# Multiplying y batch by batch in two row tiles of TensorE

## The chip, the cores and the metric

The kernel runs on one core of a Trainium2 chip. The metric is the device time of one launch in microseconds (us). Two runs of the kernel before took 425.37 and 426.58 us; their median, 425.98 us, is the time that the prediction starts from. The engines are named PE (TensorE matmuls), PEld (TensorE weight loads, which overlap PE), DVE (VectorE), ACT (ScalarE), POOL (GpSimd) and SP (SyncE, here for DMA issues only).

## What is computed

```python
# x: (64, 64, 1024) = (B, C, T); condition: (64,), values 0..15; weights: (16, 64, 64)
W = weights[condition]
y = jnp.einsum('bct,bcd->bdt', x, W)                 # one 64 x 64 matrix for each batch
x_flat = y.reshape(-1, 1024)                         # (4096, 1024)
top1 = jnp.argmax(x_flat @ gate_w.T + expert_bias, axis=-1)
base_out = jnp.einsum('bth,oh->bto', y, W_up)        # W_up: (1024, 1024)
z = jnp.einsum('nh,erh->ner', x_flat, lora_A)        # 4 experts of rank 8
delta = (z @ lora_B of expert top1) * SCALE
out = x + base_out + delta
```

All in float32. The first step, y, is what the change is about: 64 products of a batch's own 64 x 64 matrix with its 64 x 1024 slice of x.

## The kernel before

**Blocks.** The 64 batches are worked in 16 blocks of four. A block has two tiles (t = 0, 1), each of two batches that lie on 128 partitions: batch 0 of the pair on partitions 0 to 63, batch 1 on 64 to 127. Blocks 0 and 1 are partly written out on their own; blocks 2 and 3, a hardware loop over pairs (even, odd), and the last two blocks follow.

**y.** `make_y(q, par, t, h)` (L779) makes half h of y of tile t for block q, while the block ahead of it is multiplied. It has four matmuls, each with 128 columns of x as the stationary operand and `cond_pair` as the moving one. `cond_pair` is 128 x 128 and block-diagonal: the two matrices of the pair stand in its corners and zeros elsewhere, so one matmul makes y for both batches. The result, transposed (128 positions of T by 2 x 64), goes into one bank of the two-bank `y_ps`, half h into bank h. Plain float32 matmuls appear in the trace as two weight loads and two matmul records each, so a `make_y` call is 8 of each. There are four calls to a block, at four places, and 14 blocks in which y is made so (for blocks 2 to 15): 56 calls. Blocks 0 and 1 have their y from `make_first_y` (L790), which is not changed. ACT then copies the bank to SBUF (`move_y`, L522) as operand a11, a12, a21 or a22 and counts `y_summed`.

**The product with W_up.** It is done by a Strassen-like scheme: seven half-size products of a block (a11, a12, a22, s1, s2, s3, s4; `multiply`, L855), with sums of operands on POOL (L302 to L317) and operands split in a high part (ACT, L533) and a low part (DVE, L289). For an odd block and the even one ahead of it, product a22 is done in quarters (q1 to q7, L1071). In these, operands are of the type fp32r, and each matmul is one load and one matmul record. Results are added to x in SBUF by DVE (L1264, L1268, L1458) and stored by SP.

**The expert path.** DVE finds the best expert of each row in six small steps and leaves `z_parts` (L1251). PE transposes it (`turn_z`, L884), ACT copies it to `z_t` (`move_z`, L611), and PE adds the expert's part to the products' banks (`add_delta`, L875). This is done twice for each block: `turn_z` with `delta11_of` and `delta12_of` for tile 0, and `turn_second_z` with `second_delta` for tile 1. In the kernel before, the fourth `make_y` stands between `turn_second_z` and `second_delta`.

**Order.** The order on each engine is written out by hand and kept by semaphores: `y_done` (PE has made a half), `y_summed` (ACT has moved it), `z_turned`, `z_ready` (z copied), `low["s4"]` (a12 may be overwritten), `c11_out`, `u3_out` and others for banks that DVE has emptied. Each engine works in its own order, so whatever stands behind a wait waits too.

Of the kernel before, what the change touches and what calls it, by code (L numbers as in the profile page):

```python
# [5 lines left out]
def adaln_ffn_kernel(  # L6
# [62 lines left out]
    with ctx:  # L69
# [189 lines left out]
        def t_place(k, c):  # L259

            return {1: t_sb[:, c, :], 2: b12_sb[:, c, :], 3: bank_of(("b11", c)), 4: bank_of(("b21", c))}[k]

        def raw_slot(row):
            return row // OH * 2 + row % 2
# [244 lines left out]
        def _(act):  # L509
# [198 lines left out]
            def one(q):  # L708
                load_x(q + 1, 0, 0)
                round_s1(q, True)  # L710
                round_s2(q, True)
                load_x(q + 1, 0, 1)
                round_s4(q, True)
                round_s3(q, True)
                move_z(q, 1, 0, bank_c[:, 0, :])
                move_y(q + 1, 0, 0, a11)
# [4 lines left out]
                move_y(q + 1, 1, 0, a21)  # L721
                move_z(q, 1, 1, chains[0][:, 1, :])
# [6 lines left out]
                move_y(q + 1, 1, 1, a22_even)  # L729

            def even(q, g):
                load_x(q + 1, 1, 0)
                round_s1(q, True)
                round_s2(q, True)
                load_x(q + 1, 1, 1)
                round_s3(q, True)
                round_s4(q, True)
                round_even_a22(q, g)
                move_z(q, 0, 0, bank_c[:, 0, :])
                move_y(q + 1, 0, 0, a11)  # L740
                round_a11(q + 1, True)
                act.wait_ge(low["s4"], q + 1)
                move_y(q + 1, 0, 1, a12)
                round_a12(q + 1, True)
                move_y(q + 1, 1, 0, a21)
                move_z(q, 0, 1, chains[1][:, 1, :])
                move_y(q + 1, 1, 1, a22)

            def odd(q, g, closing):
                if not closing:  # L750
                    load_x(q + 1, 0, 0)
                round_s1(q, True)
                round_quarter(5, g)
                round_s2(q, True)
                round_quarter(6, g)
                round_quarter(3, g)
# [4 lines left out]
                if not closing:  # L761
                    move_y(q + 1, 0, 0, a11)
                    round_a11(q + 1, True)
                move_z(q, 1, 0, y_ps[:, 1, :])
                if not closing:
                    act.wait_ge(low["s4"], q + 1)
                    move_y(q + 1, 0, 1, a12)
                    round_a12(q + 1, True)
                    move_y(q + 1, 1, 0, a21)
                move_z(q, 1, 1, chains[0][:, 1, :])  # L770
                if not closing:
                    move_y(q + 1, 1, 1, a22_even)

# [4 lines left out]
        def _(pe):  # L778
            def make_y(q, par, t, h):  # L779
                if h == 0:  # L780
                    pe.wait_ge(x_loaded[2 * par + t], 8 * (q - par) + 16)
                    pe.wait_ge(pair_loaded[2 * par + t], 16 * (q - par) + 32)
                pe.wait_ge(y_summed, 4 * q + 2 * t + h - 1)
                for k in range(KH):
                    mm = pe.matmul(y_ps[:, h, k * P:(k + 1) * P],  # L785
                                   x_sb[:, 2 * par + t, (h * KH + k) * P:(h * KH + k + 1) * P],
                                   cond_pair[:, 2 * par + t, :], start=True, stop=True)
                mm.then_inc(y_done, 1)

# [92 lines left out]
            def turn_z(dst, q, t):  # L882
                pe.wait_ge(route_step, ROUTE_STEPS * (2 * q + t + 1))
                pe.transpose(dst, z_parts[:, :, :].rearrange("p n q -> p (n q)"), ident[:, :]).then_inc(z_turned, 1)  # L884

            def delta11_of(q, pair):
# [128 lines left out]
            def one(q):  # L1015
# [8 lines left out]
                multiply("s2", q, chain, False)  # L1024
                make_y(q + 1, 0, 0, 0)
                pe.wait_ge(p4_out, q)
# [3 lines left out]
                delta11_of(q, pair)  # L1030
                make_y(q + 1, 0, 0, 1)
                pe.wait_ge(u2_out, q + 1)
                multiply("s3", q, chain, False)
                make_y(q + 1, 0, 1, 0)
                multiply("s4", q, bank_c, True)
                delta12_of(q)
                turn_second_z(q, pair)
                make_y(q + 1, 0, 1, 1)
                pe.wait_ge(u3_out, q + 1)
                second_delta(q, chain)  # L1040

            def even(q, g):
# [72 lines left out]
            def odd(q, g, closing):  # L1115
                chain, pair = chains[1], chains[0]
                first_quarters(q, g, chain, pair)
                if closing:
                    close(q, g, chain, pair)
                    return  # L1120
                make_y(q + 1, 0, 0, 0)
                pe.wait_ge(quarter_out, quarters(g, 3))
                multiply("s1", q, bank_b, True)
                pe.wait_ge(y_summed, 4 * q + 4)
                turn_z(y_ps[:, 1, 0:P], q, 0)
# [3 lines left out]
                make_y(q + 1, 0, 0, 1)  # L1129
# [4 lines left out]
                make_y(q + 1, 0, 1, 0)  # L1134
# [4 lines left out]
                make_y(q + 1, 0, 1, 1)  # L1139
                pe.wait_ge(u3_out, q + 1)  # L1140
# [409 lines left out]
```

## Time and profile before

| | |
|---|---|
| times of the two runs | 425.37 and 426.58 us, median 425.98 |
| span of the profiled execution | 423.9 us, so 1.4 to 2.6 us of a run lie around the span |
| PE busy | 414.2 us (98%), 3003 matmul records |
| PEld busy | 393.6 us (93%) |
| DVE / ACT / POOL busy | 280.3 / 146.0 / 137.3 us |
| chain of waits that ended last | PE 92% |
| matmul records of y at L785 | 448, in 14 blocks |
| mean granted TensorE clock | 0.996 of 2.4 GHz |

A busy time is the union of the records of a group. Matmul records overlap each other, since their recorded length holds the way through the array, so the distance from start to start, not the length, tells what one costs. For weight loads the same holds. Idle time of an engine that nobody waits for costs nothing.

### The profile page before, as it was taken

To read this page: it belongs to the slowest core of one execution; us is meant where nothing else is said; L and a number is where in the kernel's file an instruction comes from. 1 tells how busy PE (TensorE), PEld (TensorE's weight loads), DVE (VectorE), ACT (ScalarE), POOL (GpSimd) and SP (SyncE) were. 2 spreads that over 40 slices of the span, in tenths; PEclk is the share of its full clock that TensorE was granted. 3 is DMA by queue.
4 is the path that set the end of the run, shared out by engine and by line. 5 is a ranking of instruction groups with operands and counts; after the bars stand their busy time and mean duration, and the time that the engine had idled before them with its cause. 6 is when DMAs were issued, how large, how long until landed. Compare 5 with 4: busy or idle time off the path is not lost.

```text
span 423.9 us, 8776 instructions
## 1 busy us (share of the span) xinstructions
PE 414.2 (98%) x3003; PEld 393.6 (93%) x3003; DVE 280.3 (66%) x605; ACT 146.0 (34%) x282; POOL 137.3 (32%) x123
## 2 busy tenths in 40 slices
PE   7998999999999999999999999999999999999997
PEld 6897998999999999999999999999999999999996
DVE  4699668586756576474675656575764756856684
ACT  5795222433223242232333233232332323323320
POOL 1488215506204080312605053050802216050430
PEclk9899999999999999999999999999999999999999
DMA  8820230503114032321125021150322212240102
GB/s 269 302 65 2 89 117 26 178 27 106 67 57 159 26 107 100 105 76 74 56 99 176 28 102 38 65 179 25 105 97 82 99 55 75 99 177 29 49 26 100
DMA packets 20991, 39.36 MB, mean 93 GB/s; under 512 B 7494, under 2 KB 7750, under 8 KB 20970
## 3 DMA queue, kind: packets, MB, share of 16 engines
q1 hardware_dynamic: 17600, 27.40, 18.3%
q10 hardware_dynamic: 3370, 11.69, 8.1%
q8 instruction: 12, 0.20, 0.2%
q14 instruction: 9, 0.07, 0.1%
HBM read 22.30 MB, written 16.78 MB: 92 GB/s over the span
## 4 chain that ended last, share of the span: by engine, by line
PE 92%; DVE 3%; DMA 1%; ACT 1%; SPq 1%; issue 1%; POOL 1%; ACTq 0%; POOLq 0%
PE bank_y L869 21%; PE bank_x L869 21%; PE y_ps L785 11%; PE bank_b L869 10%; PE bank_c L869 10%; PE bank_c L1071 5%; PE bank_b L1071 4%; DMA x_sb<-in_x_dram 1%; PE bank_x L849 1%; PE y_ps L794 1%; PE bank_x L875 1%; PE bank_b L875 1%; PE bank_y L875 1%; PE bank_c L875 1%; PE y_ps L1147 1%
## 5 line engine op out<-in xcount | busy, mean ns | idle before, releaser
L524 ACT ACTIVATE a<-y_ps 128x512 f32<-128x512 f32 x49 | 29.3, 598 | 93.4 <-PE y_ps L785 93.4
L785 PE MATMUL y_ps<-cond_pair,x_sb 128*128 128x128 f32 x448 | 59.0, 274 | 0.0
L785 PEld LDWEIGHTS y_ps<-cond_pair,x_sb 128*128 128x128 f32 x448 | 54.7, 191 | 1.2
L869 PE MATMUL bank_y<-w_s,hl_s 128*128 128x292 f32 (+1 forms) x384 | 51.4, 289 | 0.0
L869 PE MATMUL bank_x<-w_a,hl_a 128*128 128x256 f32 (+1 forms) x384 | 50.9, 288 | 0.0
L869 PEld LDWEIGHTS bank_x<-w_a,hl_a 128*128 128x128 f32 x384 | 49.5, 188 | 0.3
L304 POOL TENSOR_TENSOR s_sum<-a 128x512 f32<-128x512 f32 x9 | 11.6, 1291 | 117.3 <-ACT a L524 115.1
L869 PEld LDWEIGHTS bank_y<-w_s,hl_s 128*128 128x128 f32 x384 | 49.2, 188 | 0.1
L869 PE MATMUL bank_b<-w_s,hl_s 128*128 128x512 f32 x192 | 47.9, 398 | 0.0
L869 PE MATMUL bank_y<-w_a,hl_a 128*128 128x292 f32 x360 | 47.7, 288 | 0.0
L869 PEld LDWEIGHTS bank_y<-w_a,hl_a 128*128 128x128 f32 x360 | 46.6, 188 | 0.3
L869 PE MATMUL bank_x<-w_s,hl_s 128*128 128x292 f32 x336 | 45.2, 290 | 0.4 <-DVE hl_s L289 0.4
L304 POOL TENSOR_TENSOR s_sum<-a,a_even 128x512 f32<-128x512 f32 x7 | 9.0, 1291 | 112.4 <-ACT a_even L524 112.4
L869 PE MATMUL bank_c<-w_s,hl_s 128*128 128x512 f32 x180 | 45.0, 398 | 0.0
L869 PEld LDWEIGHTS bank_x<-w_s,hl_s 128*128 128x128 f32 x336 | 43.0, 188 | 0.6 <-issue 0.6
L869 PEld LDWEIGHTS bank_b<-w_s,hl_s 128*128 128x128 f32 x192 | 35.0, 188 | 6.9
L869 PEld LDWEIGHTS bank_c<-w_s,hl_s 128*128 128x128 f32 x180 | 32.7, 188 | 6.6 <-issue 0.2
L289 DVE TENSOR_TENSOR hl_s<-s_sum,hl_s 128x512 fp32r<-128x512 f32 x30 | 36.3, 1246 | 1.2 <-ACT hl_s L533 1.2
L289 DVE TENSOR_TENSOR hl_a<-a,hl_a 128x512 fp32r<-128x512 f32 x31 | 21.3, 689 | 18.9 <-ACT hl_a L533 18.9
L533 ACT ACTIVATE hl_s<-s_sum 128x512 fp32r<-128x512 f32 x32 | 20.2, 634 | 34.1 <-POOL s_sum L304 24.7
L1264 DVE TENSOR_TENSOR x_sb<-bank_y,x_sb 128x512 f32<-128x512 f32 x40 | 27.3, 682 | 6.0 <-PE bank_y L875 4.8
L533 ACT ACTIVATE hl_s<-a 128x512 fp32r<-128x512 f32 x32 | 19.3, 628 | 33.4 <-POOL a L312 22.5
(187 smaller groups left out, 648.3 us busy)
## 6 DMA issues: line engine op xcount, KB each, us to landing
out_dram<-x_sb SPq DMA_DIRECT2D x63, 256.0 KB, 2.0
x_sb<-in_x_dram ACTq DMA_DIRECT2D x22, 512.0 KB, 3.5
x_sb<-in_x_dram SPq DMA_DIRECT2D x10, 512.0 KB, 3.4
w_raw<-in_L_ffn_W_up_dram SPq DMA_DIRECT2D x8, 512.0 KB, 6.3
cond_pair<-in_L_cond_weights_dram SPq DMA_DIRECT2D x64, 16.0 KB, 2.2
out_dram<-x_sb SPq DMA_DIRECT2D x2, 128.0 KB, 2.0
router_sb<-in_L_ffn_lora_A_dram ACTq DMA_DIRECT2D x1, 128.0 KB
lora_b_sb<-in_L_ffn_lora_B_dram SPq DMA_DIRECT2D x1, 128.0 KB, 4.9
```

The costliest lines, as they stand in the source:

```text
L289: eng.tensor_tensor(hl[op][:, 1, :, :], by_k(src[:, :]), hl[op][:, 0, :, :].bitcast(fp32), ALU.subtract)\
L304: eng.tensor_tensor(s1_sum[:, :], a21[:, :], second[:, :], ALU.add).then_inc(s1_added, 1)
L524: act.activation(to[:, :], y_ps[:, h, :], ACT.Copy).then_inc(y_summed, 1)
L533: act.activation(hl[op][:, 0, :, :], src[:, :].rearrange("q (k n) -> q k n", n=P), ACT.Copy)\
L785: mm = pe.matmul(y_ps[:, h, k * P:(k + 1) * P], x_sb[:, 2 * par + t, (h * KH + k) * P:(h * KH + k + 1) * P], cond_pair[:, 2 * par + t, :], ...
L794: mm = pe.matmul(first_y_bank(t, h)[:, k * P:(k + 1) * P], x_sb[:, t, (h * KH + k) * P:(h * KH + k + 1) * P], cond_pair[:, t, :], start=Tr ...
L849: mm = pe.matmul(dst, hl[op][:, a, k, :], w_of[op][:, b, k, cols], start=(fresh and k == 0 and a + b == 0), stop=(k == KH - 1 and a == 1), ...
L869: mm = pe.matmul(dst, hl[op][:, a, k, :], w[:, b, k, cols], start=(fresh and k == 0 and a + b == 0), stop=(k == KH - 1 and a == 1), skip_g ...
L875: return pe.matmul(dst, z_t[t][:, :], src, start=False, stop=True, skip_group_check=True)
L1071: mm = pe.matmul(bank[:, 0, 0:QUARTER], left[:, a, k, :], right[:, b, k, :], start=(fresh and k == 0 and a + b == 0), stop=(k == 1 and a = ...
L1147: mm = pe.matmul(dst, hl["s4"][:, a, k, :], w_of["s4"][:, b, k, cols], start=(k == 0 and a + b == 0), stop=False, skip_group_check=True)
L1264: return dve.tensor_tensor(wide(x_part(par, t, half)), bank[:, :, 0:QUARTER], wide(x_part(par, t, half)), ALU.add)
```

## The change

`make_y` makes a whole tile in one call, at two places of a block (where the first and the third call stood). For each 128 columns of x it has two matmuls in place of one: one on partitions 0 to 63, with batch 0's 64 x 64 matrix, into bank 0 of `y_ps`, and one on partitions 64 to 127, with batch 1's, into bank 1. These are the two row tiles of 64 partitions of the array. `y_done` is counted after the fourth and the eighth chunk. `move_y` waits for both, and reads its half from both banks through a strided pattern. On ACT the order of the copies changes with it. In odd blocks the first transpose of z goes to columns 256 to 383 of bank 1 of the pair of banks that `delta11_of` adds to, in place of `y_ps`. Loads, stores, POOL and DVE are as before.

```diff
             def move_y(q, t, h, to):
-                act.wait_ge(y_done, 4 * q + 2 * t + h + 1)
-                act.activation(to[:, :], y_ps[:, h, :], ACT.Copy).then_inc(y_summed, 1)
+                act.wait_ge(y_done, 4 * q + 2 * t + 2)
+                act.activation(to[:, :].rearrange("q (k b d) -> q k b d", b=2, d=D),
+                               y_ps[:, :, h * QUARTER:(h + 1) * QUARTER].rearrange("q b (k d) -> q k b d", d=D),
+                               ACT.Copy).then_inc(y_summed, 1)
...
             def even(q, g):
...
-                move_z(q, 0, 0, bank_c[:, 0, :])
                 move_y(q + 1, 0, 0, a11)
-                round_a11(q + 1, True)
+                move_z(q, 0, 0, bank_c[:, 0, :])
                 act.wait_ge(low["s4"], q + 1)
                 move_y(q + 1, 0, 1, a12)
+                round_a11(q + 1, True)
                 round_a12(q + 1, True)
                 move_y(q + 1, 1, 0, a21)
+                move_y(q + 1, 1, 1, a22)
                 move_z(q, 0, 1, chains[1][:, 1, :])
-                move_y(q + 1, 1, 1, a22)
...
-            def make_y(q, par, t, h):
-                if h == 0:
-                    pe.wait_ge(x_loaded[2 * par + t], 8 * (q - par) + 16)
-                    pe.wait_ge(pair_loaded[2 * par + t], 16 * (q - par) + 32)
-                pe.wait_ge(y_summed, 4 * q + 2 * t + h - 1)
-                for k in range(KH):
-                    mm = pe.matmul(y_ps[:, h, k * P:(k + 1) * P],
-                                   x_sb[:, 2 * par + t, (h * KH + k) * P:(h * KH + k + 1) * P],
-                                   cond_pair[:, 2 * par + t, :], start=True, stop=True)
-                mm.then_inc(y_done, 1)
+            def make_y(q, par, t):
+                pe.wait_ge(x_loaded[2 * par + t], 8 * (q - par) + 16)
+                pe.wait_ge(pair_loaded[2 * par + t], 16 * (q - par) + 32)
+                pe.wait_ge(y_summed, 4 * q + 2 * t)
+                for k in range(KC):
+                    for b in range(2):
+                        rows = slice(b * C, (b + 1) * C)
+                        mm = pe.matmul(y_ps[:, b, k * D:(k + 1) * D],
+                                       x_sb[rows, 2 * par + t, k * P:(k + 1) * P],
+                                       cond_pair[rows, 2 * par + t, b * D:(b + 1) * D], start=True, stop=True)
+                    if k % KH == KH - 1:
+                        mm.then_inc(y_done, 1)
...
             def even(q, g):
...
                 multiply("s2", q, chain, False)
-                make_y(q + 1, 1, 0, 0)
+                make_y(q + 1, 1, 0)
                 pe.wait_ge(c12_out, q)
                 turn_z(bank_c[:, 0, 0:P], q, 0)
                 pe.wait_ge(c22_out, q)
                 multiply("s1", q, bank_b, True)
                 delta11_of(q, pair)
-                make_y(q + 1, 1, 0, 1)
                 pe.wait_ge(u2_out, q + 1)
                 multiply("s3", q, chain, False)
-                make_y(q + 1, 1, 1, 0)
+                make_y(q + 1, 1, 1)
                 multiply("s4", q, bank_c, True)
                 delta12_of(q)
                 turn_second_z(q, pair)
-                make_y(q + 1, 1, 1, 1)
                 pe.wait_ge(u3_out, q + 1)
                 second_delta(q, chain)
```

Blocks 1 and the odd ones are changed likewise.

Where instructions moved, two places matter. First PE, from the end of s3 to the end of an odd block (L884 and L893 are the transposes of z there, L875 and L884 of the changed kernel add the expert's part). Before:

```order
L1071 MATMUL bank_c<-w_a,hl_a 128x256 x6
L785 MATMUL y_ps<-cond_pair,x_sb 128x128 x4
L869 MATMUL bank_c<-w_s,hl_s 128x512 x12
L875 MATMUL bank_c<-lora_b_hl,z_t 128x512
L884 MATMUL bank_x<-ident,z_parts 128x128
L785 MATMUL y_ps<-cond_pair,x_sb 128x128 x4
L875 MATMUL bank_y<-lora_b_hl,z_t 128x256 x2
L875 MATMUL bank_b<-lora_b_hl,z_t 128x512
```

In the changed kernel:

```order
L1081 MATMUL bank_c<-w_a,hl_a 128x256 x6
L793 MATMUL y_ps<-cond_pair,x_sb 128x64 x16
L878 MATMUL bank_c<-w_s,hl_s 128x512 x12
L884 MATMUL bank_c<-lora_b_hl,z_t 128x512
L893 MATMUL bank_x<-ident,z_parts 128x128
L884 MATMUL bank_y<-lora_b_hl,z_t 128x256 x2
L884 MATMUL bank_b<-lora_b_hl,z_t 128x512
```

The four matmuls of y between the transpose of z and the products that read its copy have gone to the place ahead of s4, and all 16 of the tile have 64 moving columns.

Second ACT, from the first copy of z of an even block to its last copy (`a<-y_ps` are the copies of y, `hl_a<-a` the roundings of a11 and a12). Before:

```order
L611 ACTIVATE z_t<-bank_c 128x128 [waits delta12,z_turned]
L524 ACTIVATE a<-y_ps 128x512 [waits y_done]
L533 ACTIVATE hl_a<-a 128x512 [waits product_a11,y_summed]
L524 ACTIVATE a<-y_ps 128x512 [waits y_done,low_s4]
L533 ACTIVATE hl_a<-a 128x512 [waits product_a12,y_summed]
L524 ACTIVATE a<-y_ps 128x512 [waits y_done]
L611 ACTIVATE z_t<-bank_y 128x128 [waits delta22,z_turned]
L524 ACTIVATE a<-y_ps 128x512 [waits y_done]
```

In the changed kernel:

```order
L528 ACTIVATE a<-y_ps 128x512 [waits y_done]
L617 ACTIVATE z_t<-bank_c 128x128 [waits delta12,z_turned]
L528 ACTIVATE a<-y_ps 128x512 [waits y_done,low_s4]
L539 ACTIVATE hl_a<-a 128x512 [waits product_a11,y_summed]
L539 ACTIVATE hl_a<-a 128x512 [waits product_a12,y_summed]
L528 ACTIVATE a<-y_ps 128x512 [waits y_done] x2
L617 ACTIVATE z_t<-bank_y 128x128 [waits delta22,z_turned]
```

The first copy of z stands behind a copy of y now, the rounding of a11 behind the wait for `low["s4"]`, and the last copy of y ahead of the second copy of z.

## Rows read from the trace of the kernel before

**Rows 1.** The page's head and its first part: busy us and share.

```profile
span 423.9 us, 8776 instructions
PE 414.2 (98%) x3003; PEld 393.6 (93%) x3003; DVE 280.3 (66%) x605; ACT 146.0 (34%) x282; POOL 137.3 (32%) x123
```

**Rows 2.** Busy time by stretch: stretch, its length, busy us (records) of each engine.

```profile
60.00:120.00 60.00, 58.45 (x423) 55.17 (x422) 42.84 (x84) 20.32 (x39) 20.29 (x16) 1.00 0.23 78
120.00:180.00 60.00, 60.00 (x437) 57.02 (x436) 36.53 (x86) 18.42 (x35) 18.15 (x15) 1.00 0.26 91
...
360.00:405.00 45.00, 45.00 (x326) 42.65 (x326) 28.65 (x67) 14.42 (x28) 13.10 (x12) 1.00 0.23 84
```

**Rows 3.** Waits, 60 to 396 us, PEld: us in total, times, longest.

```profile
PEld bank_x L884 <- issue: 1.5, 1, 1.5
PEld bank_x L869 <- issue: 0.6, 1, 0.6
```

**Rows 4.** Timeline of weight loads in an even and an odd block: start, length.

```profile
196.60 0.14 PEld L884 LDWEIGHTS bank_y<-ident,z_parts 128*128 128x128 f32 x1
196.83 0.97 PEld L785 LDWEIGHTS y_ps<-cond_pair,x_sb 128*128 128x128 f32 x8
197.72 0.30 PEld L875 LDWEIGHTS bank_x<-lora_b_hl,z_t 128*128 128x128 f32 x2
...
210.83 0.98 PEld L785 LDWEIGHTS y_ps<-cond_pair,x_sb 128*128 128x128 f32 x8
211.73 2.61 PEld L869 LDWEIGHTS bank_b<-w_s,hl_s 128*128 128x128 f32 x12
```

**Rows 5.** Groups by line and form: busy us, mean ns, idle before.

```profile
L785 PE MATMUL y_ps<-cond_pair,x_sb 128*128 128x128 f32 x448 | 59.0, 274 | 0.0
...
L785 PEld LDWEIGHTS y_ps<-cond_pair,x_sb 128*128 128x128 f32 x448 | 54.7, 191 | 1.2
```

**Rows 6.** The same view in two stretches that end after one and two loads.

```profile
82.61 0.19 PEld L869 LDWEIGHTS bank_x<-w_s,hl_s 128*128 128x128 f32 x1 [0.59 <-issue]
...
82.61 0.30 PEld L869 LDWEIGHTS bank_x<-w_s,hl_s 128*128 128x128 f32 x2 [0.59 <-issue]
```

**Rows 7.** Timeline of loads about the transposes of the 36 router rows.

```profile
6.31 0.47 PEld L803 LDWEIGHTS bank_x<-ident,w_raw 128*128 128x128 f32 x4
6.95 0.14 PEld L810 LDWEIGHTS bank_y<-ident,router_sb 36*128 36x128 f32 x1 [0.17 <-issue]
...
6.95 0.57 PEld L810 LDWEIGHTS bank_y<-ident,router_sb 36*128 36x128 f32 x8 [0.17 <-issue]
7.68 0.42 PEld L803 LDWEIGHTS y_ps<-ident,w_raw 128*128 128x128 f32 x4 [0.16 <-issue]
```

**Rows 8.** Timeline, end of an even block: the second z on PE and ACT.

```profile
196.83 0.27 PE L884 MATMUL bank_y<-ident,z_parts 128*128 128x128 f32 x1
...
197.13 0.28 ACT L611 ACTIVATE z_t<-bank_y 128x128 fp32r<-128x128 f32 x1 [2.49 <-PE bank_y L884]
```

**Rows 9.** Timeline: PE's answer to a semaphore from DVE.

```profile
39.42 0.23 DVE L1251 TENSOR_TENSOR z_parts<-z_sel,z_parts 128x64 f32<-128x64 f32 x1
...
39.76 0.14 PEld L884 LDWEIGHTS y_ps<-ident,z_parts 128*128 128x128 f32 x1 [1.11 <-issue]
```

**Rows 10.** Timeline of ACT and DVE in an even block.

```profile
187.06 0.63 ACT L533 ACTIVATE hl_a<-a 128x512 fp32r<-128x512 f32 x1
...
194.05 0.60 ACT L524 ACTIVATE a<-y_ps 128x512 f32<-128x512 f32 x1 [2.64 <-PE y_ps L785]
...
184.13 1.28 DVE L289 TENSOR_TENSOR hl_s<-a,hl_s 128x512 fp32r<-128x512 f32 x2
...
187.72 0.69 DVE L289 TENSOR_TENSOR hl_a<-a,hl_a 128x512 fp32r<-128x512 f32 x1 [1.71 <-ACT hl_a L533]
189.02 0.69 DVE L1268 TENSOR_TENSOR x_sb<-bank_b,x_sb 128x512 f32<-128x512 f32 x1 [0.60 <-PE bank_b L869]
```

**Rows 11.** Timeline, end of block 1: second z.

```profile
74.51 0.14 PEld L884 LDWEIGHTS bank_x<-ident,z_parts 128*128 128x128 f32 x1 [1.54 <-issue]
...
74.54 1.00 PEld L785 LDWEIGHTS y_ps<-cond_pair,x_sb 128*128 128x128 f32 x8
```

More of the change, by code:

```diff
@@ L261, in t_place, with odd_z @@
             return {1: t_sb[:, c, :], 2: b12_sb[:, c, :], 3: bank_of(("b11", c)), 4: bank_of(("b21", c))}[k]
+        def odd_z(pair):
+            return pair[:, 1, QUARTER:QUARTER + P]
         def raw_slot(row):
@@ L714, in one @@
                 round_s3(q, True)
+                move_y(q + 1, 0, 0, a11)
                 move_z(q, 1, 0, bank_c[:, 0, :])
-                move_y(q + 1, 0, 0, a11)
-                round_a11(q + 1, True)
                 act.wait_ge(low["s4"], q + 1)
                 move_y(q + 1, 0, 1, a12)
+                round_a11(q + 1, True)
                 round_a12(q + 1, True)
                 move_y(q + 1, 1, 0, a21)
+                move_y(q + 1, 1, 1, a22_even)
                 move_z(q, 1, 1, chains[0][:, 1, :])
@@ L728, in one @@
                 round_fine(4)
-                move_y(q + 1, 1, 1, a22_even)
             def even(q, g):
@@ L738, in even @@
                 round_even_a22(q, g)
+                move_y(q + 1, 0, 0, a11)
                 move_z(q, 0, 0, bank_c[:, 0, :])
-                move_y(q + 1, 0, 0, a11)
-                round_a11(q + 1, True)
                 act.wait_ge(low["s4"], q + 1)
                 move_y(q + 1, 0, 1, a12)
+                round_a11(q + 1, True)
                 round_a12(q + 1, True)
                 move_y(q + 1, 1, 0, a21)
+                move_y(q + 1, 1, 1, a22)
                 move_z(q, 0, 1, chains[1][:, 1, :])
-                move_y(q + 1, 1, 1, a22)
             def odd(q, g, closing):
@@ L760, in odd @@
                 round_odd_a22(q, g)
-                if not closing:
+                if closing:
+                    move_z(q, 1, 0, y_ps[:, 1, :])
+                else:
                     move_y(q + 1, 0, 0, a11)
-                    round_a11(q + 1, True)
-                move_z(q, 1, 0, y_ps[:, 1, :])
-                if not closing:
+                    move_z(q, 1, 0, odd_z(chains[0]))
                     act.wait_ge(low["s4"], q + 1)
                     move_y(q + 1, 0, 1, a12)
+                    round_a11(q + 1, True)
                     round_a12(q + 1, True)
                     move_y(q + 1, 1, 0, a21)
+                    move_y(q + 1, 1, 1, a22_even)
                 move_z(q, 1, 1, chains[0][:, 1, :])
-                if not closing:
-                    move_y(q + 1, 1, 1, a22_even)
             one(1)
@@ L884, in turn_z, with turn_odd_z @@
                 pe.transpose(dst, z_parts[:, :, :].rearrange("p n q -> p (n q)"), ident[:, :]).then_inc(z_turned, 1)
+            def turn_odd_z(dst, q):
+                pe.wait_ge(route_step, ROUTE_STEPS * (2 * q + 1))
+                pe.matmul(dst, z_parts[:, :, :].rearrange("p n q -> p (n q)"), ident[:, :], is_transpose=True,
+                          start=False, stop=True, skip_group_check=True).then_inc(z_turned, 1)
             def delta11_of(q, pair):
@@ L1024, in one @@
                 multiply("s2", q, chain, False)
-                make_y(q + 1, 0, 0, 0)
+                make_y(q + 1, 0, 0)
                 pe.wait_ge(p4_out, q)
@@ L1030, in one @@
                 delta11_of(q, pair)
-                make_y(q + 1, 0, 0, 1)
                 pe.wait_ge(u2_out, q + 1)
                 multiply("s3", q, chain, False)
-                make_y(q + 1, 0, 1, 0)
+                make_y(q + 1, 0, 1)
                 multiply("s4", q, bank_c, True)
@@ L1120, in odd @@
                     return
-                make_y(q + 1, 0, 0, 0)
+                make_y(q + 1, 0, 0)
                 pe.wait_ge(quarter_out, quarters(g, 3))
                 multiply("s1", q, bank_b, True)
-                pe.wait_ge(y_summed, 4 * q + 4)
-                turn_z(y_ps[:, 1, 0:P], q, 0)
+                turn_odd_z(odd_z(pair), q)
                 pe.wait_ge(quarter_out, quarters(g, 6))
@@ L1128, in odd @@
                 delta11_of(q, pair)
-                make_y(q + 1, 0, 0, 1)
                 pe.wait_ge(u2_out, q + 1)
@@ L1133, in odd @@
                 q4(g)
-                make_y(q + 1, 0, 1, 0)
+                make_y(q + 1, 0, 1)
                 pe.wait_ge(quarter_out, quarters(g, 4))
```

2 lines of the change are left out of this document (removed).

## The prediction, made before the changed kernel was run

> **What bounds the kernel now.** I began with the page's head and engine shares [rows 1]: PE is busy 414.2 of 423.9 us, every other engine far less. A share is a mean over stages, so next came the busy times by stretch [rows 2]. From 120 us on PE is busy in every microsecond of a stretch (60.00 of 60.00, 45.00 of 45.00). Between 60 and 396 us, where all 56 calls of y lie, the weight loads waited twice, 1.5 and 0.6 us [rows 3]. So in the steady blocks nobody makes PE wait: PE time added there is paid in full, PE time taken away is gained in full, and slack won on ACT, POOL or DVE is worth nothing. The chain of waits says the same, 92% of it being PE.
>
> Since PE's records overlap, what y costs is the distance between starts. The loads of a y call begin at 210.83 and the next product's at 211.73 [rows 4], so 8 load and matmul pairs take 0.90 us, 0.112 us each; 448 of them [rows 5] take 50.4 us. That is the stake of the change.
>
> **Is y bound by its streaming or by its loads?** The change halves what is streamed, 128 columns to 64, but a load still has 128 columns. There are two loads of the same length as those of y (0.19 us) after PE had sat idle, with nothing streaming ahead of them: one load ends at 0.19 us, two at 0.30 [rows 6]. The second starts 0.11 us after the first. So a load alone allows one pair in 0.11 us, y's present pace, and streaming less can't beat that. Nor do fewer rows shorten a load: that of 36 partitions (L810) lasts 0.14 us [rows 7], as a 128-partition transpose's does [rows 4]. (Eight of them in 0.57 us are (0.57 - 0.14)/7 = 0.061 us apart; transposes load faster than products do.)
>
> **The change, part by part.**
>
> 1. *The pairs.* 28 tiles x 8 chunks x 2 halves x 2 records = 896 pairs replace 448. Each row tile has 16 loads per y tile, as the whole array had. If the two row tiles load at the same time, a place takes 16 x 0.112 = 1.79 us, what two calls took: plus or minus nothing. No row shows two loads at once. One end is no overlap at all: 448 more pairs x 0.112 = 50.2 us. Below, the nearest row with a short stream is 0.061 us to a pair [rows 7]; 16 such spacings for 32 pairs would be 0.98 us, 0.81 less at each of 28 places, -22.7 us. I take nil, since the load rate of [rows 6] holds for each tile by itself and the row tiles use separate partitions. The Trainium skill, "TensorEngine Tiling (Array Packing)", Key Properties, says that different tiles can run weight loads and matmuls in parallel; by it the term is this nil, and no run here shows it.
>
> 2. *Going into the row tiles and out.* The router's transposes (36 partitions) are the only matmuls on fewer than 128 rows. Ahead of their first load the loads pause 0.17 us and behind the last 0.16 us, for "issue", nothing that the profile can name [rows 7]; between calls on 128 rows there is no such pause [rows 4]. I read it as the array emptying at a change of shape. Each place pays it twice. Lower end 0; upper end 0.33 plus twice the overlap that is lost (0.19 - 0.11 = 0.08), 0.49 us. I take 0.41, the middle of the two sums with a pause: 28 x 0.41 = +11.5 us (0 to 13.7).
>
> 3. *The cover of the second z.* Its transposes' matmul starts at 196.83 and ends at 197.10; ACT copies z from 197.13 to 197.41 [rows 8]. PE needs 0.11 us from a semaphore to its load (39.65 to 39.76) [rows 9], so `second_delta` could load at 197.52. It loads at 197.72 [rows 4], because the fourth y call, loading from 196.83, hides the whole trip. That call is gone from there: the load that could begin at 196.83 begins at 197.52. PE is in order, and the next block's a11 stands behind it. +0.69 us x 14 blocks = +9.7 us (0.6 to 0.8 each). ACT is free then, as the two copies of y ahead of it (0.60 each [rows 10]) fit beside s4.
>
> 4. *The late z of block 1.* There the transpose waited for DVE 1.5 us [rows 11]; the y pairs that now stand ahead of it take 0.9 of that. -1.0 us with the lost load.
>
> 5. *Waits that could take over.* a11's rounding stands behind a copy of y that waits for `low["s4"]`. In an even block that is signalled at 185.41, earlier than ACT comes to it. The rounding ended at 187.69 and now ends after 0.9 us more of y and a copy more (0.60), at 189.2; DVE's low part of a11 follows, and its next work, which s1 released at 189.02, comes 0.9 us later too [rows 10]. Nothing on PE hangs on it for 7 us. The second y call needs a12's copy out, which is ready some 3 us ahead. In odd blocks q7 still covers the first z. Zero for these, and zero for the two calls moved.
>
> Sum: 0 + 11.5 + 9.7 - 1.0 = +20.2 us. On the profiled span, 423.9 to 444.1; on the median of the runs, 2.1 us above the span, 425.98 to **446 us**. With the bounds of steps 2 and 3, and up to 32 x 0.061 - 1.79 = 0.16 us a place if a pair can't be issued faster than in rows 7 (+4.5), this case spans 434 to 454.
>
> **The rivals.**
>
> - *The loads don't overlap* (slower still). A load may only go when the matmul ahead of it in program order has started, and that one waits for its own load, on the same tile. All rows agree with such an order as well as with free tiles: a load starts with the matmul before it (both at 196.83) [rows 4, 8]. Then step 1 costs 50.2 us: 425.98 + 50.2 + 20.2 = 496 us.
> - *No pause at the change of shape.* The pauses of rows 7 stand in the opening, where transfers were landing too. Without step 2: 425.98 + 9.7 - 1.0 = 435 us, on the 2% line.
> - *Loads of 64 rows are quick and paired* (faster). If a product's load on half the rows takes what a transpose's takes, each place saves 0.81 us from the moment that loads overlap: with the pause 446 - 22.7 = 423 us, without it 412 us. Without the pause it is over 2% faster once the spacing of loads inside one row tile is under 0.074 us ((1.79 - 17.2 / 28) / 16, with 17.2 = 8.7 + 8.5). Against it speaks that a transpose's load is as long on 36 rows as on 128. The skill's tiling page, Theoretical Speedup, promises up to twofold for a contraction of 64 or less. Halving the 50.4 us would give 425.98 - 25.2 + 8.7 = 409 us without a pause, 421 with one. [Rows 6] speak against it, as that gain is in streaming.
> - *The change doesn't do what it says:* if the stages weren't in separate row tiles, the pairs would run one by one, which is the first rival's time less the pauses, 485 us; I hold it within that rival.
>
> **Chances.** Forecast (446) 0.46; loads one after another (485 to 500) 0.24; no pause (435) 0.10; quick loads with a pause (423) 0.08; quick loads without (412) 0.12. For 80% I take the forecast's whole span, the case without a pause and the serial case with its upper bound, 434 to 500 us, which leaves out the two quick cases. The forecast's own range is 434 to 454. Two per cent, about what a measurement tells from no change here, is 417.5 to 434.5 us: faster 0.12, the same 0.08 + half of 0.10 = 0.13, slower 0.75.
>
> **What would show it.** In the changed profile: loads of y with 64 rows, and a whole place in about 1.8 us (step 1), or 3.6 (serial), or 1.0 (quick); idle of PEld for "issue" ahead of the first y load and behind the last, 0.17 us or so (step 2); PE idle 0.6 to 0.7 us ahead of `second_delta`, released by ACT's copy of z, 14 times (step 3); block 1's wait shorter (step 4). Wrong would be a pause of another size, a place of y that takes an in-between time (some loads overlap), or a wait of PE for `y_summed`, which I hold for impossible by 3 us.

## The result and the profile after

The changed kernel took 444.16 and 445.32 us, median 444.74 us. Against the kernel before that is a ratio of 1.0445 (95% interval 1.0401 to 1.0489): slower, as forecast, 1.3 us below the predicted 446. The profiled execution's own time was 444.16 us, with a span of 442.3 us against 423.9, so 18.4 us more.

Head and engine shares of the page, to be held against [rows 1]:

```profile
span 442.3 us, 9656 instructions
PE 427.7 (97%) x3451; PEld 397.5 (90%) x3451; DVE 261.1 (59%) x605; ACT 134.9 (31%) x282; POOL 126.9 (29%) x123
```

PE has 448 more records, as there are two matmuls for each one of y. Its busy time rises by 13.5 us, the loads' by 3.9 us, though the loads have 448 more records too: many of them must run beside each other. By stretch (stretch, length, then busy us and records of PE, PEld, DVE, ACT and POOL, granted clock, DMA share, GB/s), to be held against [rows 2]:

```profile
120.00:180.00 60.00, 59.08 (x495) 54.76 (x494) 32.23 (x83) 15.14 (x33) 14.65 (x14) 1.00 0.23 78
```

In its steady stretches PE was busy in every microsecond before. Now it idles 0.92 us of 60, at an unchanged granted clock of 1.00 (the level of 2.4 GHz). So the time went to gaps and not to a slower clock. The waits from 60 to 410 us (us in total, times, longest), first of PEld, against [rows 3]:

```profile
PEld bank_y L884 <- issue: 5.5, 7, 0.8
PEld bank_x L884 <- issue: 4.6, 6, 0.8
PEld y_ps L793 <- issue: 1.8, 12, 0.2
PEld bank_x L878 <- issue: 0.8, 4, 0.2
PEld bank_y L893 <- issue: 0.7, 1, 0.7
```

and of PE:

```profile
PE bank_y L884 <- ACT z_t L617: 3.2, 7, 0.5
PE bank_x L884 <- ACT z_t L617: 2.7, 6, 0.5
PE bank_y L893 <- DVE z_parts L1258: 0.3, 1, 0.3
```

L884 is `add_delta`, the product that reads the copy of z, and L617 ACT's copy: it waits once in each of 14 blocks, 13 times up to 410 us and once more, for block 14, at 414. L793 is y; only some of its pauses are long enough for this view. L878 is the first product behind the turn of the loop over pairs of blocks. L893 is the transpose of z, which waits for DVE once, in block 2.

A place of y in the timeline of loads (start, length), against [rows 4]. The last line is the same view in a stretch that ends at 218.09:

```profile
217.13 0.79 PEld L1081 LDWEIGHTS bank_b<-w_a,hl_q 128*128 128x128 f32 x6
218.05 1.86 PEld L793 LDWEIGHTS y_ps<-cond_pair,x_sb 64*128 64x128 f32 x32
219.98 0.30 PEld L878 LDWEIGHTS bank_b<-w_s,hl_s 128*128 128x128 f32 x2
...
218.05 0.19 PEld L793 LDWEIGHTS y_ps<-cond_pair,x_sb 64*128 64x128 f32 x2
```

Two loads of y have begun within 0.04 us: one in each row tile. Loads of y on whole rows begin 0.11 us apart. The 32 loads end after 1.86 us, and from the first of them to the first load behind them it is 1.93 us. Two calls on whole rows took 16 x 0.112 = 1.79 us. Ahead of the first, the six loads of L1081 last 0.79 us together and 0.19 each, so they start (0.79 - 0.19) / 5 = 0.12 us apart. From the first of them to y it is 218.05 - 217.13 = 0.92 us, which is 0.2 us more than 6 x 0.12.

By line and form, against [rows 5]:

```profile
L793 PEld LDWEIGHTS y_ps<-cond_pair,x_sb 64*128 64x128 f32 x896 | 52.2, 188 | 4.0 <-issue 1.8
```

A load on 64 rows lasts 188 ns and one on 128 lasted 191: half the rows save nothing, as [rows 7] had let one expect of 36.

The second z of an odd block (PEld, PE and ACT from the timeline), against [rows 8]:

```profile
232.52 0.14 PEld L893 LDWEIGHTS bank_x<-ident,z_parts 128*128 128x128 f32 x1
232.75 0.27 PE L893 MATMUL bank_x<-ident,z_parts 128*128 128x128 f32 x1
233.05 0.28 ACT L617 ACTIVATE z_t<-bank_x 128x128 fp32r<-128x128 f32 x1 [2.19 <-PE bank_x L893]
233.44 0.30 PEld L884 LDWEIGHTS bank_y<-lora_b_hl,z_t 128*128 128x128 f32 x2 [0.79 <-issue]
...
234.06 0.30 PEld L878 LDWEIGHTS bank_x<-w_a,hl_a 128*128 128x128 f32 x2 [0.21 <-issue]
```

This is the predicted chain, step by step: the copy ends at 233.33, 0.11 us later the load starts. No load lies between 232.66 and 233.44. The last line is something that was not predicted: at the turn of the loop PEld stands idle for 0.21 us more.

**A clean measure: the period.** The same transpose comes once in each pair of blocks of the hardware loop. Before, two periods apart:

```profile
223.96 0.14 PEld L884 LDWEIGHTS bank_x<-ident,z_parts 128*128 128x128 f32 x1
...
323.30 0.14 PEld L884 LDWEIGHTS bank_x<-ident,z_parts 128*128 128x128 f32 x1
```

After, two periods behind the 232.52 above:

```profile
337.52 0.14 PEld L893 LDWEIGHTS bank_x<-ident,z_parts 128*128 128x128 f32 x1
```

Two periods are 99.34 us before and 105.00 after, so one is 49.67 and 52.50: 2.83 us more for each pair of blocks. The experiments below are read with the same measure, since it does not hold the opening, the end or blocks 1 and 2, and repeats closely (52.49 and 52.51 for the two after). The period ahead of the loop's first turn (the transposes at 127.64 and 180.00) is 52.35, or 0.15 us less: that is what the pause at the turn adds.

### The profile page after: what moved, and what is told of

The parts are those of the page before. It is cut to its first block, busy times and chain, and to the rows that moved or that the text cites. A ratio compares the mean times of both kernels' runs of the same rounds, so it can differ in the third digit from the quotient of the medians.

```text
span 442.3 us, 9656 instructions
## 1 busy us (share of the span) xinstructions
PE 427.7 (97%) x3451; PEld 397.5 (90%) x3451; DVE 261.1 (59%) x605; ACT 134.9 (31%) x282; POOL 126.9 (29%) x123
## 4 chain that ended last, share of the span: by engine, by line
PE 91%; DVE 3%; DMA 2%; issue 1%; ACT 1%; SPq 1%
PE bank_y L878 21%; PE bank_x L878 20%; PE y_ps L793 12%; PE bank_b L878 10%; PE bank_c L878 10%; PE bank_c L1081 5%; PE bank_b L1081 3%; DMA w_raw<-in_L_ffn_W_up_dram 1%; PE bank_x L858 1%; PE bank_x L884 1%; PE bank_y L884 1%; ACT z_t L617 1%; PE bank_b L884 1%; PE bank_c L884 1%; PE y_ps L1154 1%
## 5 line engine op out<-in xcount | busy, mean ns | idle before, releaser
L793 PE MATMUL y_ps<-cond_pair,x_sb 64*128 64x64 f32 x896 | 56.1, 275 | 0.0
L793 PEld LDWEIGHTS y_ps<-cond_pair,x_sb 64*128 64x128 f32 x896 | 52.2, 188 | 4.0 <-issue 1.8
L878 PE MATMUL bank_x<-w_a,hl_a 128*128 128x256 f32 (+1 forms) x384 | 51.3, 289 | 0.0
L878 PE MATMUL bank_y<-w_s,hl_s 128*128 128x292 f32 (+1 forms) x384 | 50.9, 288 | 0.0
L878 PEld LDWEIGHTS bank_x<-w_a,hl_a 128*128 128x128 f32 x384 | 49.3, 188 | 1.0 <-issue 0.8
L878 PEld LDWEIGHTS bank_y<-w_s,hl_s 128*128 128x128 f32 x384 | 49.3, 188 | 0.1
L878 PE MATMUL bank_b<-w_s,hl_s 128*128 128x512 f32 x192 | 48.0, 399 | 0.0
L878 PE MATMUL bank_y<-w_a,hl_a 128*128 128x292 f32 x360 | 47.7, 288 | 0.0
L878 PEld LDWEIGHTS bank_y<-w_a,hl_a 128*128 128x128 f32 x360 | 46.6, 188 | 0.3
L878 PE MATMUL bank_c<-w_s,hl_s 128*128 128x512 f32 x180 | 45.3, 400 | 0.0
L878 PE MATMUL bank_x<-w_s,hl_s 128*128 128x292 f32 x336 | 44.6, 288 | 0.0
L878 PEld LDWEIGHTS bank_x<-w_s,hl_s 128*128 128x128 f32 x336 | 43.1, 188 | 0.0
L878 PEld LDWEIGHTS bank_b<-w_s,hl_s 128*128 128x128 f32 x192 | 35.4, 190 | 7.2
L878 PEld LDWEIGHTS bank_c<-w_s,hl_s 128*128 128x128 f32 x180 | 32.6, 188 | 7.5 <-issue 0.2
L1275 DVE TENSOR_TENSOR x_sb<-bank_c,x_sb 128x512 f32<-128x512 f32 x16 | 11.1, 691 | 40.5 <-PE bank_c L884 39.2
L539 ACT ACTIVATE hl_s<-s_sum 128x512 fp32r<-128x512 f32 x32 | 19.3, 626 | 38.6 <-DMA out_dram<-x_sb 38.5
L1271 DVE TENSOR_TENSOR x_sb<-bank_x,x_sb 128x512 f32<-128x512 f32 x40 | 27.4, 686 | 4.7 <-PE bank_x L884 2.9
```

The costliest lines, as they stand in the source:

```text
L539: act.activation(hl[op][:, 0, :, :], src[:, :].rearrange("q (k n) -> q k n", n=P), ACT.Copy)\
L793: mm = pe.matmul(y_ps[:, b, k * D:(k + 1) * D], x_sb[rows, 2 * par + t, k * P:(k + 1) * P], cond_pair[rows, 2 * par + t, b * D:(b + 1) * D ...
L878: mm = pe.matmul(dst, hl[op][:, a, k, :], w[:, b, k, cols], start=(fresh and k == 0 and a + b == 0), stop=(k == KH - 1 and a == 1), skip_g ...
L1271: return dve.tensor_tensor(wide(x_part(par, t, half)), bank[:, :, 0:QUARTER], wide(x_part(par, t, half)), ALU.add)
L1275: return dve.tensor_tensor(x_part(par, t, half), bank[:, 0, :], x_part(par, t, half), ALU.add)
```

## The experiments

The theory is the prediction's: two causes, the pauses at the row tiles and the lost cover of the second z, and nothing from the pairs themselves. The rivals are that one of the two is the whole loss, that the pairs cost something because the loads hardly overlap, or that a mere new place for y costs something.

### y on whole rows at the two places

The kernel after with y as before, eight matmuls of 128 rows and 128 columns a tile. ACT's copy reads one bank in a row again, in place of the strided pattern. Places, order and waits stay as changed.

```diff
 def make_y(q, par, t):
...
                 for k in range(KC):
-                    for b in range(2):
-                        rows = slice(b * C, (b + 1) * C)
-                        mm = pe.matmul(y_ps[:, b, k * D:(k + 1) * D],
-                                       x_sb[rows, 2 * par + t, k * P:(k + 1) * P],
-                                       cond_pair[rows, 2 * par + t, b * D:(b + 1) * D], start=True, stop=True)
+                    mm = pe.matmul(y_ps[:, k // KH, k % KH * P:(k % KH + 1) * P],
+                                   x_sb[:, 2 * par + t, k * P:(k + 1) * P],
+                                   cond_pair[:, 2 * par + t, :], start=True, stop=True)
```

> The changed kernel with its two places and its order, but y made on all 128 rows with the block-diagonal matrix again (8 matmuls a tile, no row tiles). Theory (each place pays about 0.4 us at the changes of shape, and the pairs of the row tiles cost what the whole array's do, within 0.06 us a place): 28 x 0.35 = 9.7 less, 0.9 of it taken back since a transpose behind the place no longer hides in the pause: 436. Rival (no pause; the whole loss is the missing cover of z and waits): 444.7. Rival (row tiles gain and something else loses more): above 446.

Measured: 435.59 us, ratio 1.0209 (1.0188 to 1.0230). So row tiles by themselves cost 444.74 - 435.59 = 9.2 us, and the rest of the loss is there without them. ACT's changed pattern has no part in it: a copy of y takes 599 ns in both kernels. The timeline:

```profile
223.28 0.78 PEld L1077 LDWEIGHTS bank_c<-w_a,hl_a 128*128 128x128 f32 x6
223.99 1.88 PEld L789 LDWEIGHTS y_ps<-cond_pair,x_sb 128*128 128x128 f32 x16
225.78 0.30 PEld L874 LDWEIGHTS bank_c<-w_s,hl_s 128*128 128x128 f32 x2
```

Six loads ahead of y in 0.71 us instead of 0.92, the place in 1.79 instead of 1.93: 0.35 us is what a visit to the row tiles costs. The waits of PEld in this kernel. Not shown are the seven of L880 in `bank_x` (5.4 us) and two ahead of transposes of z in blocks 1 and 2 (0.4 and 0.9 us):

```profile
PEld bank_y L880 <- issue: 5.3, 7, 0.8
PEld bank_x L874 <- issue: 0.9, 4, 0.2
```

No line of y is left; the waits for z's copy and at the loop's turn are all there, so they belong to the places and not to the row tiles.

### The second z transposed ahead of s4

The kernel after, with the second transpose of z ahead of s4 in blocks 2 to 14, so that s4 covers the trip over ACT.

```diff
                 make_y(q + 1, 1, 1)
+                turn_second_z(q, pair)
                 multiply("s4", q, bank_c, True)
                 delta12_of(q)
-                turn_second_z(q, pair)
                 pe.wait_ge(u3_out, q + 1)
```

(Odd blocks likewise.)

> The changed kernel, but in the even and odd blocks the second transpose of z stands ahead of s4, so s4's 2.8 us hide ACT's copy of z. Theory (the cover of the second z is gone, 0.69 us a block): 13 blocks x 0.69 = 9.0 us less than the changed kernel's 444.7, so 435.8, and the idle of PE ahead of the first of the three last products of a block gone in all blocks but block 1. Rival (the time lies all in the row tiles, and PE would idle elsewhere): 444.7. Second rival: the z of these blocks isn't ready so early, and a wait for DVE ahead of the transpose takes the place of the old one: 440 to 445.

Measured: 440.94 us, ratio 1.0342 (1.0309 to 1.0375). The theory's 435.8 was missed; the second rival, a wait for DVE, had it. The waits of PE:

```profile
PE bank_y L893 <- DVE z_parts L1258: 5.0, 7, 3.4
PE bank_y L884 <- ACT z_t L617: 0.5, 1, 0.5
```

The 5.9 us of waiting for ACT have come down to 0.5 (block 1, which is not edited), but in their stead the transpose waits 5.0 us for DVE. Most of it is block 2, on DVE's timeline:

```profile
91.35 1.89 DVE L1392 TENSOR_TENSOR w_q<-rebuilt_b,w_q 128x512 fp32r<-128x512 f32 x3
...
97.92 0.68 DVE L1258 TENSOR_TENSOR z_parts<-z_sel,z_parts 128x64 f32<-128x64 f32 x1
```

DVE splits weights until 93.24 and works on a queue of other things behind that, so z is ready only at 98.60, while PE could have taken it from 95.2 on. I had looked whether the transpose could stand earlier for PE and ACT, and not when its input is made.

### The same on whole rows

Both edits above together:

```diff
-                    for b in range(2):
...
+                    mm = pe.matmul(y_ps[:, k // KH, k % KH * P:(k % KH + 1) * P],
...
+                turn_second_z(q, pair)
                 multiply("s4", q, bank_c, True)
```

> Both edits together: whole rows, and the second transpose of z ahead of s4 in the even and odd blocks. Only the two places and ACT's order are left of the change. Theory (two causes that add): 436 - 9.0 = 427, the kernel before within 1 us or so. Rival (making y in two places costs by itself, a wait for y_summed or the late rounding of a11): 430 or more.

Measured: 435.40 us, ratio 1.0221 (1.0193 to 1.0249); 427 was missed for the same reason:

```profile
PE bank_y L889 <- DVE z_parts L1254: 5.9, 7, 3.4
```

Without the pauses PE comes earlier still and waits 5.9 us for DVE. One wait has been exchanged for another of the same size, so these two runs say little on the price of the lost cover. That called for a place between the two.

### The second z transposed in the middle of s4

The kernel after, with the transpose behind six of s4's twelve matmuls, in blocks 3 to 14; blocks 1 and 2 stay as they are. Six matmuls still cover ACT, and DVE has 1.3 us more.

```diff
-            def multiply(op, q, bank, fresh):
+            def multiply(op, q, bank, fresh, between=None):
...
                 for k in range(KH):
+                    if k == 2 and between:
+                        between()
...
-                multiply("s4", q, bank_c, True)
+                multiply("s4", q, bank_c, True, lambda: turn_second_z(q, pair))
                 delta12_of(q)
-                turn_second_z(q, pair)
```

> The changed kernel, with the second transpose of z in the middle of s4 (after 6 of its 12 matmuls) in blocks 3 to 14; blocks 1 and 2 stay. e1 had it ahead of s4, where even blocks wait 0.4 us for DVE's z and block 2 waits 3.4. Here 1.4 us of s4 stand ahead of it, more than those 0.4, and 1.4 us behind it, more than the 0.69 that the copy needs. Theory (the missing cover): 12 blocks x 0.69 = 8.3 less than 444.7, and the slow turn of the loop (0.2 us, four times) gone with it: 435.6 to 436.4. Rival (the gain of e1, 3.8 us, is all there is): 441.

Measured: 435.00 us, ratio 1.0192 (1.0152 to 1.0232). Its timeline of loads:

```profile
228.46 1.23 PEld L880 LDWEIGHTS bank_c<-w_s,hl_s 128*128 128x128 f32 x6
229.73 0.14 PEld L895 LDWEIGHTS bank_x<-ident,z_parts 128*128 128x128 f32 x1
229.96 1.23 PEld L880 LDWEIGHTS bank_c<-w_s,hl_s 128*128 128x128 f32 x6
231.22 0.19 PEld L886 LDWEIGHTS bank_c<-lora_b_hl,z_t 128*128 128x128 f32 x1
231.45 0.42 PEld L886 LDWEIGHTS bank_y<-lora_b_hl,z_t 128*128 128x128 f32 x2
...
231.92 3.19 PEld L880 LDWEIGHTS bank_x<-w_a,hl_a 128*128 128x128 f32 x24
```

Neither the delta nor the next block's first product waits for anything. With the wait for z the 0.2 us at the turn of the loop has gone too. The time is just under the expected 435.6 to 436.4. The same transpose one period later:

```profile
280.73 0.14 PEld L895 LDWEIGHTS bank_x<-ident,z_parts 128*128 128x128 f32 x1
```

### The same on whole rows: both causes away

```diff
-                    for b in range(2):
...
+                    mm = pe.matmul(y_ps[:, k // KH, k % KH * P:(k % KH + 1) * P],
...
-                multiply("s4", q, bank_c, True)
+                multiply("s4", q, bank_c, True, lambda: turn_second_z(q, pair))
```

> The same on whole rows (no row tiles): e2's 435.6 less the same 8.3 to 9.1 gives 426.5 to 427.3. If the two causes are all of the loss, this is the kernel before again within 1.3 us, still with y at two places. Rival (y at two places costs something of its own): 429 or more.

Measured: 426.28 us, ratio 1.0001 (0.9973 to 1.0028). With both causes taken out, the change's two places of y cost and bring nothing that can be measured. One period:

```profile
222.80 0.14 PEld L891 LDWEIGHTS bank_x<-ident,z_parts 128*128 128x128 f32 x1
...
272.50 0.14 PEld L891 LDWEIGHTS bank_x<-ident,z_parts 128*128 128x128 f32 x1
```

The four corners as medians and as period of a pair of blocks (distance of the transposes into `bank_x`, as read above; on whole rows with the second z behind s4 they stand at 228.65 and 279.90):

| | y in row tiles | y on whole rows | difference |
|---|---|---|---|
| second z behind s4 | 444.74 us, 52.50 | 435.59 us, 51.25 | 9.2 us, 1.25 |
| second z in the middle of s4 | 435.00 us, 51.00 | 426.28 us, 49.70 | 8.7 us, 1.30 |
| difference | 9.7 us, 1.50 | 9.3 us, 1.55 | |
| kernel before | | 425.98 us, 49.67 | |

The two causes add: each costs the same whether the other is there or not. The medians carry 1 to 2 us of doubt each (the interval of the kernel after, 0.0044 either way, is 1.9 us), so the periods show it more sharply.

### Batch after batch in the row tiles

Is the overlap of the two tiles' loads what keeps the pairs at nil? The kernel after, with all eight chunks of batch 0 ahead of those of batch 1. The work is the same and only neighbours in PE's queue change.

```diff
-                for k in range(KC):
-                    for b in range(2):
+                for b in range(2):
+                    for k in range(KC):
...
-                    if k % KH == KH - 1:
-                        mm.then_inc(y_done, 1)
+                    mm.then_inc(y_done, 1)
```

> The changed kernel, but each place does all eight chunks of batch 0 and then all eight of batch 1, in place of alternating. In the changed kernel the pairs are 0.054 us apart. Theory (a load in one row tile takes 0.107 us as on the whole array, and the pace of 0.054 comes from one load running in each tile, which needs neighbours in program order on different tiles): pairs 0.107 to 0.112 us apart, 32 x 0.108 - 1.73 = 1.7 us more a place, 28 x 1.7 = +48, so 493. Rival (a load of 64 rows takes 0.054 us by itself, whatever the tile): 444.7. Rival (PE looks far ahead and pulls batch 1's loads beside batch 0's): 445 to 450.

Measured: 485.90 us, ratio 1.1417 (1.1387 to 1.1447), against an expected 493. One place on the timeline of loads, then two stretches of 0.4 us in it (stretch, length, PEld busy and records that touch it, clock, DMA):

```profile
204.50 3.25 PEld L793 LDWEIGHTS y_ps<-cond_pair,x_sb 64*128 64x128 f32 x32
207.82 0.14 PEld L892 LDWEIGHTS bank_c<-ident,z_parts 128*128 128x128 f32 x1
```

```profile
205.00:205.40 0.40, 0.40 (x6) 1.00 0.00 0
205.83:206.23 0.40, 0.40 (x9) 1.00 0.00 0
```

Such a stretch of the kernel after, inside a place of alternating batches:

```profile
218.80:219.20 0.40, 0.40 (x10) 1.00 0.00 0
```

A load lasts 0.19 us, so (0.40 + 0.19) / 0.112 = 5.3 records touch such a stretch at the pace of one tile, and twice that where both tiles load. With one tile at work, loads on 64 rows still come only every 0.11 us; both tiles are at work only where batch 1's first loads run beside batch 0's last three. In the place read here that is for 7 spacings of 31. It takes 3.32 us instead of 1.93; 28 x 1.39 = 38.9 us is the 38.6 us between the spans (480.9 and 442.3). So the pairs cost nothing more only because neighbouring instructions sit in different tiles. The first rival, loads one after another, holds in this kernel for 24 of 31 spacings; the 7 short ones save about 7 x 0.055 x 28 = 11 us, and the expectation, which had none of them, was 7 us too high.

### Half the moving columns, whole rows

Is y bound by loads? The kernel before, with 64 moving columns in place of 128; batch 1's half of y is not made in the steady blocks.

```diff
-                    mm = pe.matmul(y_ps[:, h, k * P:(k + 1) * P],
+                    mm = pe.matmul(y_ps[:, h, k * P:k * P + D],
...
-                                   cond_pair[:, 2 * par + t, :], start=True, stop=True)
+                                   cond_pair[:, 2 * par + t, 0:D], start=True, stop=True)
```

> The kernel before with 64 moving columns in each matmul of y in place of 128; batch 1's half of y isn't made in the steady blocks (the rest of the work is all there). As many loads, of as many columns and rows, half the streaming. Theory (y is bound by its weight loads): pairs still 0.112 us apart or 0.107 at the least, so 424 to 426. Rival (y is bound by streaming, and row tiles only failed to gain because they have as many streams in all): pairs 0.06 us apart, 448 x 0.05 = 22 less, 404.

Measured: 425.45 us, ratio 0.9999 (0.9975 to 1.0022).

```profile
213.39 0.98 PEld L785 LDWEIGHTS y_ps<-cond_pair,x_sb 128*128 128x128 f32 x8
214.29 0.30 PEld L869 LDWEIGHTS bank_y<-w_s,hl_s 128*128 128x128 f32 x2
```

Eight pairs still take 0.90 us, and the rival's 404 us did not come. The streaming that the change halves had been free.

### One small matmul more, on 64 rows or on 128

Is the pause a price of changing shape, or of a short matmul ahead of y? To the kernel before one matmul of 64 columns is added ahead of the first and the third call of y, at 28 places; its result is overwritten at once. It is on 64 rows in one kernel and on 128 in the other.

```diff
                 pe.wait_ge(y_summed, 4 * q + 2 * t + h - 1)
+                if h == 0:
+                    pe.matmul(y_ps[:, 0, 0:D], x_sb[0:64, 2 * par + t, 0:P], cond_pair[0:64, 2 * par + t, 0:D],
+                              start=True, stop=True)
```

> The kernel before with one small matmul more ahead of y's first call of each tile (28 of them, two load and matmul pairs each), on 64 rows and 64 moving columns, its output overwritten by y. To be read against e9, the same on 128 rows. Theory (the array empties at each change of shape, 0.41 us for a way in and out): 28 x (0.41 + 2 x 0.11) = 17.6 more than before's 426, so 443.6. Rival (the pauses of the changed kernel belong to pairs of tiles, or to y_ps, not to a change of shape): as e9, 432.

> The kernel before with the same small matmul on all 128 rows, 64 moving columns. Two more pairs at 28 places: 28 x 2 x 0.112 = 6.3 more, 432.3 under every theory. The difference of e8 and e9 is the price of the change of shape alone, 11.4 us by theory, 0 by the rival.

Measured: 439.91 us, ratio 1.0338 (1.0295 to 1.0380), on 64 rows; 431.70 us, ratio 1.0147 (1.0095 to 1.0199), on 128. The loads with 64 rows:

```profile
216.77 0.79 PEld L1074 LDWEIGHTS bank_b<-w_a,hl_q 128*128 128x128 f32 x6
217.70 0.29 PEld L785 LDWEIGHTS y_ps<-cond_pair,x_sb 64*128 64x128 f32 x2
218.06 0.97 PEld L788 LDWEIGHTS y_ps<-cond_pair,x_sb 128*128 128x128 f32 x8
218.95 0.19 PEld L872 LDWEIGHTS bank_b<-w_s,hl_s 128*128 128x128 f32 x1
```

and with 128:

```profile
213.08 0.79 PEld L1074 LDWEIGHTS bank_b<-w_a,hl_q 128*128 128x128 f32 x6
213.80 0.31 PEld L785 LDWEIGHTS y_ps<-cond_pair,x_sb 128*128 128x128 f32 x2
214.03 0.97 PEld L788 LDWEIGHTS y_ps<-cond_pair,x_sb 128*128 128x128 f32 x8
214.92 0.19 PEld L872 LDWEIGHTS bank_b<-w_s,hl_s 128*128 128x128 f32 x1
```

From the six loads ahead to the first behind it is 2.18 us with 64 rows and 1.84 with 128. Of the 0.34 us, 0.21 lie ahead of the small matmul (0.93 - 0.72) and 0.13 behind it (0.36 - 0.23). The pause is there with a single matmul in a single tile, so it belongs to the change of shape, in both directions, and not to the pairs of tiles. 28 x 0.34 = 9.5 us; the profiled spans (439.6 and 430.4) differ by 9.2 and the medians by 8.2. The kernel on 64 rows was expected at 443.6 and the two 11.4 us apart. That was some 3 us too high: 0.41 us for the round trip accounts for 28 x 0.07 = 2 us of it, and the rest lies within the doubt of the medians.

The small matmul on whole rows has two loads; 28 x 2 x 0.112 = 6.3 us agrees with its 431.70 - 425.50 = 6.2 us over the kernel before run beside it.

## Why the prediction was right

The forecast case came, its four terms with their signs, 446 against 444.74 us. The miss is mainly step 2, which was 1.7 us too high. That it is no larger is in part luck, since the terms that were not foreseen (in points 4 and 5) nearly cancel one another, and a median of two runs is not known to 1.3 us. The low end of the forecast's range was added up 0.6 us too high: no pause and 0.6 us a block give 433.4, not 434. Step by step:

1. *The pairs: nil.* Right. Both tiles load at once, 32 pairs in 1.93 us with the way out of the tiles, and the three kernels on this, half the columns (nothing gained), batch after batch (38.6 us lost) and whole rows (a place of 1.79 us), close it from all sides. The bound of 0.061 us to a pair, which widened the own range upward, was not needed: pairs went by at 0.056, half of 0.112. The quick loads failed: a load on 64 rows takes as long as on 128. [Rows 11] had shown that two loads can begin 0.03 us apart even on whole rows, a transpose's and the first of y, though the prediction says that no row shows two at once. The Trainium skill, "TensorEngine Tiling (Array Packing)", Key Properties, says that different tiles can load and multiply in parallel; the trace agrees, with two loads begun within 0.04 us. The up to twofold of the same page of the Trainium skill (Theoretical Speedup) did not come: 28 places of 1.93 us instead of 1.79. The Trainium skill, "TensorE: Matmul & The Clock Gate", LDWEIGHTS, says that a load's time goes by its columns and not by its rows; the trace agrees, with 188 ns on 64 rows against 191 on 128.
2. *Going into row tiles and out.* The mechanism was right and the size 17% high: 0.35 us a place, 9.8 us, for 0.41 and 11.5. It costs 0.21 us in and 0.14 out, and of the two sums that I took the middle of, the lower one, the bare idle time of [rows 7] (0.33), was the nearer. The Trainium skill, "TensorEngine Tiling (Array Packing)", Key Properties, says that a change of tiling mode drains the engine. The kernels with one small matmul agree so far as they show a pause at each change, 0.34 us for the round trip; that it is a drain they can't show.
3. *The cover of the second z.* Right in place and size: 0.79 us of PEld's idle is 0.70 us more than the usual 0.09 between two such loads. With 13 of these and a shorter one in block 2 (0.62 idle) that is 9.6 us against 9.7 predicted. On PE the profile shows only 0.5 us of idle a time, not the 0.6 to 0.7 that were to show it. Taking the wait away in 12 blocks gained 9.7 us in row tiles and 9.3 on whole rows. That is more than 12 x 0.70 = 8.4; four turns of the loop (point 5) make it 9.0, and the rest is within the doubt of the medians.
4. *The late z of block 1.* Its wait went, but block 2's transpose now comes 0.7 us late on PEld (0.3 on PE), for DVE, which is not in step 4. The two came to -0.8 in place of -1.0. The second wait of [rows 3], 0.6 us for DVE in block 2, has gone as well. Step 4 doesn't have it.
5. *Not foreseen.* Where PE has just waited for z ahead of the turn of the loop, PEld idles 0.2 us, four times, which adds 0.15 us to the period each time: +0.6. Before, eight matmuls of y stood in the queue there. What exactly makes the 0.2 us was not tested alone; that it comes and goes with the wait is shown by all four corners. In the other direction, in 8 blocks the first transpose of z now stands right behind a place in row tiles and its load hides in the way out, about 0.11 us each, -0.9:

```profile
87.35 0.14 PEld L893 LDWEIGHTS bank_c<-ident,z_parts 128*128 128x128 f32 x1
87.36 2.67 PEld L878 LDWEIGHTS bank_b<-w_s,hl_s 128*128 128x128 f32 x12
```

The sum 0 + 9.8 + 9.6 - 0.8 - 0.6 + 0.6 - 0.9 = 17.7 us stands against 18.4 between the spans. The 0.7 us left over lie outside the steady blocks and have no cause shown; the spans of the two runs after differ by 1.2 us themselves (442.3 and 443.5). For one pair of blocks the sum is 4 x 0.35 - 0.11 + 2 x 0.70 + 0.15 = 2.84 us against a measured 2.83.

None of the waits that step 5 of the prediction put at zero appeared: PE never waited for `y_summed`, for a11 or for a12.

What was wrong was the first theory of two experiments, the early transposes, by 5 and 8 us. The clue was in [rows 11]: DVE's z was late in block 1 already.

## What to carry to other kernels

Before a matmul is split over row tiles, ask what sets its pace. Here halving the moving columns alone changed nothing, as loads set it, and two tiles gave just the old pace back, and that only while neighbours in the queue alternated between them. Each visit cost 0.35 us here, so a visit must hold enough matmuls that gain. And when calls that stand between a producer and its reader are gathered elsewhere, price the trip they covered, over every engine on it; to cover it anew, look first when its input is ready.

## What the runs showed of the hardware that I had not expected

- PE takes up loads of the other row tile only where they are close in its queue: with eight chunks of a batch in a row only 7 of 31 spacings of the place read were short (0.05 to 0.06 us in place of 0.11). Batch 1's first load, at 205.90, went ahead of just the last three of batch 0.
- In the row tiles the two loads of a pair start 6 to 7 ns apart and the next pair 0.105 us later, so two small loads cost 0.112 us together, the same as one on whole rows.
- The way out of the row tiles hides a transpose's load: the next load on whole rows starts 0.01 us after it, where such neighbours are 0.11 apart otherwise.
- A wait of PE just ahead of the loop's turn cost 0.15 us beyond itself (PEld idle 0.2 us), four times of four; turns without such a wait show no idle time in the view of waits.
